# A new timetable for GpSimd's gathers in a recommender kernel with self-attention (one Trainium2 core)

## What is computed

```python
embed_x = emb_table[X + offsets[None, :]]          # 2048 x 39 x 64, the gather
att = embed_x
for i in range(3):
    q, k, v = att @ WQ[i], att @ WK[i], att @ WV[i]    # two heads of 32
    attn = softmax(einsum('bihd,bjhd->bhij', q, k))
    att = relu(einsum('bhij,bjhd->bihd', attn, v) + att @ WR[i])
att_output = relu(att.reshape(2048, 2496) @ Wlin)
h = relu(embed_x.reshape(2048, 2496) @ W1 + b1)
h = relu(h @ W2 + b2)
y = sigmoid(att_output + relu(h @ W3 + b3))
```

## Time and profile before

| | |
|---|---|
| three runs | 2014.25, 2020.08, 2020.95 us (median 2020.08, mean 2018.4) |
| the profiled execution | 2015.38 us |
| its span, first to last instruction | 2013.2 us |
| TensorE, VectorE, ScalarE, GpSimd busy | 95%, 84%, 68%, 45% of the span |
| mean granted clock of TensorE | 0.992 of full |

### The profile page before, as it was taken

The page is one execution under the profiler, slowest core; times in us unless marked ns, Lnnn a source line. Parts: engine busy times, 40 slices in busy tenths (PEclk is TensorE's granted clock), DMA queues, the critical chain, the costliest instruction groups (busy, mean ns, idle before and its releaser), DMA issues.

```text
span 2013.2 us, 105402 instructions
## 1 busy us (share of the span) xinstructions
PE 1903.5 (95%) x44960; PEld 1688.1 (84%) x44960; DVE 1691.6 (84%) x3771; ACT 1370.4 (68%) x3993; POOL 900.1 (45%) x949
## 2 busy tenths in 40 slices
PE   1598999999999999999999999999999999999998
PEld 0487888888888888888888888888888888888887
DVE  4476989888898888889888898988889888888987
ACT  2365767777777677777767677677767777777675
POOL 7553354544545454454544445454454545444000
PEclk9899999999999999999999999999999999999998
DMA  4111111111111111111111111111111111111000
GB/s 137 43 28 25 32 27 32 29 30 32 29 33 29 31 30 30 31 28 33 28 31 30 30 34 28 32 30 30 31 30 33 28 32 28 31 31 25 21 19 17
DMA packets 67862, 64.73 MB, mean 32 GB/s; under 512 B 24056, under 2 KB 54792, under 8 KB 67400
## 3 DMA queue, kind: packets, MB, share of 16 engines
q1 hardware_dynamic: 47432, 37.52, 6.4%
q0 software_dynamic: 19968, 20.49, 5.3%
HBM read 27.24 MB, written 0.01 MB: 14 GB/s over the span
## 4 chain that ended last, share of the span: by engine, by line
PE 87%; DVE 5%; issue 3%; POOL 2%; ACT 2%; another core or an unknown queue 1%; DMA 0%; ACTq 0%
PE SV L478 20%; PE Ob L495 14%; PE X L464 13%; PE X L457 8%; PE X L459 5%; PE X L458 5%; PE Mb L432 3%; PE Mb L433 3%; PE Mb L434 3%; PE Ob L457 3%; PE Ob L459 3%; PE Ob L458 3%; POOL emb L355 2%; PE Ob L423 2%; PE Mb L450 1%
## 5 line engine op out<-in xcount | busy, mean ns | idle before, releaser
L355 POOL DMA_INDIRECT emb<-L_rec_emb_table,idx_t x624 | 653.0, 1046 | 727.3 <-PE Ob L495 531.6
L742 DVE TENSOR_REDUCE den<-sd 103x16 f32<-103x624 f32 x384 | 308.2, 803 | 212.5 <-ACT sd L615 188.9
L478 PE MATMUL SV<-yv,xs 64*39 64x142 f32 x12288 | 454.5, 286 | 12.0 <-ACT v_sb L618 10.0
L478 PEld LDWEIGHTS SV<-yv,xs 64*39 64x39 f32 x12288 | 344.9, 113 | 52.4 <-issue 15.7
L722 DVE TENSOR_REDUCE mx<-SV 103x8 f32<-103x312 f32 x768 | 333.1, 475 | 33.0 <-PE SV L478 17.2
L495 PEld LDWEIGHTS Ob<-pt,v_sb 39*32 39x32 f32 x12288 | 271.7, 106 | 96.1 <-issue 95.8
L599 ACT ACTIVATE xs<-Ob 128x312 f32<-128x312 f32 x256 | 110.4, 431 | 346.4 <-PE Ob L495 345.3
L464 PE MATMUL X<-ident,pn 103*103 103x103 f32 x3072 | 342.7, 254 | 0.0
L332 POOL COPY xs<-embT 64x256 f32<-64x256 f32 x300 | 239.9, 800 | 211.8 <-ACT embT L559 77.6
L727 DVE TENSOR_TENSOR sd<-SV,mx 103x312 f32<-103x312 f32 x768 | 331.5, 474 | 0.1
L495 PE MATMUL Ob<-pt,v_sb 39*32 39x39 f32 x12288 | 324.9, 198 | 6.2 <-issue 5.9
(11 more groups left out here) (81 smaller groups left out, 2757.7 us busy)
## 6 DMA issues: line engine op xcount, KB each, us to landing
v_x<-v_sb SPq DMA_DIRECT2D x768, 39.0 KB
emb<-L_rec_emb_table,idx_t POOLq DMA_INDIRECT x624
xs<-L_rec_W SPq DMA_DIRECT2D x19, 256.0 KB
w<-L_rec_W SPq DMA_DIRECT2D x1, 512.0 KB
idx_in<-r_X SPq DMA_DIRECT2D x1, 312.0 KB, 4.0
b_b<-L_rec_b SPq DMA_DIRECT2D x1, 256.0 KB
b_b<-L_rec_b SPq DMA_DIRECT2D x1, 128.0 KB
w_b<-L_rec_W SPq DMA_DIRECT2D x1, 128.0 KB
```

Source lines behind the costliest of these rows:

```text
L355: nc.gpsimd.indirect_dma_start(out=emb[:, n % ER, f % 2 * D:(f % 2 + 1) * D], out_offset=None, in_=table, in_offset=bass.IndirectOffsetOnA ...
L478: last = nc.tensor.matmul(SV[64 * b:64 * b + F, at:at + YR], x_pair(u, e, p), yv[64 * e:64 * e + D, l, p, :], start=True, stop=True, skip_ ...
L742: nc.vector.tensor_reduce(den[:], pe_sb[:], AX.X, ALU.add).then_inc(den_ready, 1)
```

## The change

The two tables of fields are changed, tile 0 gets a table of its own for the copies, and in steps 0 to 2 of tile 0 POOL waits for the scores of the step before (`sv_ps`) before it gathers:

```diff
-    FIELDS_AT = [2, 2, 2, 2, 2, 2, 2, 2, 1, 2, 0, 2, 0, 2, 2, 0, 2, 2, 2, 0, 2, 2, 2, 2]
-    FIRST_FIELDS_AT = [10] + 9 * [2] + [1, 2, 1, 2, 2, 1, 2]
+    FIELDS_AT = [2, 2, 2, 2, 3, 2, 2, 2, 0, 2, 0, 2, 0, 2, 2, 0, 2, 2, 2, 0, 2, 2, 2, 2]
+    FIRST_FIELDS_AT = 3 * [4] + 5 * [3] + [0, 2, 0, 2, 2, 0, 2, 2, 2]
     SHUFFLE_AT = {8: 0, 10: 1, 12: 2, 15: 3, 19: 4}
+    FIRST_SHUFFLE_AT = {8: 0, 10: 1, 13: 2, 19: 3, 21: 4}
...
             for s in range(TOTAL):
                 t, ts = tile_step(s)
+                if s <= PV_AT:
+                    at_least(pool, sv_ps, 2 * s)
                 at_least(pool, o_ps, s - PV_AT)
                 for f in fields_at(s)[1]:
                     gather(fields_at(s)[0], f)
-                shuffles = ts in SHUFFLE_AT and t + 1 < TILES
-                if shuffles:
+                shuffle_at = SHUFFLE_AT if t else FIRST_SHUFFLE_AT
+                if ts in shuffle_at and t + 1 < TILES:
                     for back in range(min(4, s + 1)):
                         for f in fields_at(s - back)[1]:
                             landed(pool, fields_at(s - back)[0], f)
-                    shuffle_for(t + 1, SHUFFLE_AT[ts])
+                    shuffle_for(t + 1, shuffle_at[ts])
```

## The result

The changed kernel takes 1991.97 us (median of four runs, 1987.01 to 1997.73), the kernel before beside it 2018.65: a ratio of 0.987 (95% interval 0.9852 to 0.9889), 27 us. The forecast was 1988.0 with a range of 1975 to 2005, faster by over 0.3%. That is right. The profiled execution took 1989.57 us, 25.8 less than that of before, where the sum had said 30.4. The last experiments set a limit to what it is right about: on another chip, the third of those used here, the same change is worth 0.2%.

A forecast was written before the change was run, and what follows sets the result against it. TensorE was taken to bound the kernel (busy 95%, 87% of the chain), stalled by gather issues. Terms -14.7 + 8.4 - 8.0 - 0.7 + 1.0 - 18.1 + 1.75 = -30.4 us gave 1985.0, predicted median 1988 us, range 1975 to 2005.

The forecast's parts named there:

- Step 9, tiles 1 to 14: Without step 8's gather, copies end earlier and step 9's gathers end ahead of TensorE's burst: -14.7 us.
- Third gather in step 4: Step 8's gather, moved to step 4, ends at phase 3.30 inside the burst: 0.60 each, +8.4 us over 14 tiles.
- Tile 0, steps 0 and 1: Four gathers a step, waiting for the previous step's scores, replace fourteen issued back to back: -8.0 us.
- Tile 0, steps 9 to 23: Copies placed after their last chunk, so gathers no longer go out in bunches: -18.1 us, step 21 priced separately.
- Step 21: Tile 0's one step keeping gathers and copies together: ScalarE's cast for tile 1 comes late, +1.75 us.
- Tile 0, steps 2 to 7: Step 2: -0.7 us; third gathers in steps 3 to 7 end ahead of the burst, costing only +1.0, in step 3.
- The signs: Expected trace marks, including step 4 at about 5.4 us and PE's unnamed wait on L495 from 23.3 to about 10.
- the first: Rival: the burst's gaps are not the gathers' doing, so time stays at 2018 to 2020 us; 5%.
- A third gather costs 1.26 everywhere: Rival: step 9's stall price in all 19 steps with a third gather, sum -15.9, 2002.5 us; 10%.
- The slower case: Third gathers in step 4 and tile 0's steps 3 to 7 cost 2.4 us or more each, over 0.3% slower; 3%.
- while GpSimd issues a gather, TensorE's densest stream of small instructions does not get on: Claimed mechanism at burst L495 (64 tiny matmuls): loss grows with the issue's reach, 0.48 to 1.26 us a step.
- the rule that spoke against the change: Only VectorE and GpSimd share a port pair, so TensorE and ScalarE never wait there; sum would be about nothing.

The follow-up runs named there:

- the change's steady part alone: Kernel before with only the new FIELDS_AT table for tiles 1 to 15, tile 0 as before: 2009.97 us, ratio 0.9956.
- the kernel with the new tile 0 alone: Changed kernel with the old FIELDS_AT, keeping tile 0's tables and the sv_ps waits: 2001.39 us, ratio 0.9908.

## Why the prediction was right, and where not

- **Step 9, tiles 1 to 14**: -14.7 forecast, -15.6 measured. The early copies and the second gather ahead of the burst are as described; the change's steady part alone shows it.
- **Third gather in step 4**: +8.4 forecast, +10.7 measured, 0.76 each for 0.60. That it costs was right, the straight line between two rows too low: they were taken from second gathers, and a third costs more at the same phase. That the cost goes by how far the issue reaches into the burst was wrong, as the third gather in step 3 shows.
- **Step 10**, for which nothing was counted, fell by 3.0 us (from 71.6). 1.4 of them are a lower clock in one tile: in tile 7 the kernel before ran this step at a granted clock of 0.74 and took 6.44 us. In most others it is about 0.15 shorter, as steps behind a stalled one are longer elsewhere too (step 4 above, behind step 3's third gather); why is not shown. With 3.0 us more in small differences, tiles 1 to 14 come to -10.9, where -6.3 was forecast.
- **Tile 0, steps 0 and 1**: 10.49 us forecast, 10.73 measured.
- **Tile 0, steps 9 to 23**: 75.1 us forecast (91.46-18.1+1.75), 76.1 measured. Step 21 is the late one, 6.73 us, and the clock is 1.00 in the whole stretch, where it was 0.94.
- **Tile 0, steps 2 to 7**: here the working failed. "Where the pair takes 0.94 each, the third runs from phase 1.91 to 2.85, ahead of the burst at 2.98: nothing" gave +1.0 for steps 3 to 7; steps 3 to 8 rose by 4.9 us, from 29.3 to 34.2. The third gathers make 3.3 of it, 0.5 to 0.7 in each of their five steps and 0.2 in step 8 behind them: so it is in the kernel with the new tile 0 alone, whose clock is 1.00 there (32.54). The other 1.7 are this execution's: step 3 ran at a granted clock of 0.74 and took 6.43 us with TensorE busy throughout, and step 4 took 6.18, where the kernel with tile 0 alone has 5.51 and 5.48. The four gathers of step 2 were priced at nothing beside a gain of 0.7; the step rose by 1.1, to 7.44. The variant with the third gather in step 3 shows the same without tile 0: ending before the burst does not make a third gather free.
- **The sum**: span -25.6 us = 3.5 before the first mark, -17.0 in tile 0, -10.9 in tiles 1 to 14, -1.2 behind. The 3.5 are chance: three kernels with the same instructions there reach the first mark at 68.14, 70.47 and 74.11 us. That the total came within 5 us is partly luck: tile 0 gave 7.0 us less than the terms for it, and tiles 1 to 14 gave 4.6 more, most of it from steps that no term stood for.
- **The signs**: PE's unnamed wait was to fall to about 10 us and fell to 14.2; step 4 takes 5.6 and not 5.4. The late cast behind step 21 is there, 1.8 us for 1.75.

Of the rivals, the first falls on the first chip (the loss moved with the gathers, three times). "A third gather costs 1.26 everywhere" falls by its size (0.58 and 0.76, with the step behind it 0.76 and 0.85), but is right that the stretch ahead of the burst is not free. The slower case, from 2.4 us for each third gather on, is further off still. What I read as a property of the machine, "while GpSimd issues a gather, TensorE's densest stream of small instructions does not get on", is one of a chip: the same instructions at the same phases leave the burst whole on the third. It is too narrow even on the first, where a stop can begin after the issue has ended, VectorE waits with TensorE, and in tile 0 ScalarE does (last section). On the third chip the rule that spoke against the change, from the Trainium skill, "SBUF — State Buffer", section "SBUF: two separate sides", agrees with the rows, and its sum of "about nothing" is about what the change is worth there (0.2%). On the first chip that sum fails; whether the rule does is not shown, as no trace places the stall at the ports of the SBUF.

What stays open: what in the first chip couples a gather to TensorE and its signals. It is hardly the way that one program was loaded, since all six traces counted with it have late rises of `sv_ps`, each of another kernel, and none of the eight others has; but the kernels ran on one chip at a time, so another condition of that time is not excluded. What the number of bytes does is open too: the kernel with a quarter of them ran only where there is no stall. So is why a third gather costs at phase 2.86 and a second at 2.72 does not.

## What to carry to other kernels

Cut the profile at a mark in each step and compare the same step's sum over all tiles: a loss of one microsecond in one step of 24 is plain there, and invisible in an engine's share. Keep a queue that waits for its own transfers away from work that must start early, but price a moved instruction by rows with the same number of neighbours, not only the same phase. And profile the kernel before on a second chip before a stall without a releaser is called a rule: here 27 us of gain on one chip are 3 on another.

## What the hardware showed that was not expected

- The same program differs by 56 us between chips (2019.25 and 1963.21). The granted clock differs by too little for it: its mean is 0.992 on the first and 0.997 on the third. The two profiled executions of the kernel before differ by 50.8: 26.5 us lie in tile 0 (145.5 and 119.0) and 24.9 in tiles 1 to 14 (1670.9 and 1646.0), with 0.7 the other way outside them. Of the 24.9 step 9 makes 11.0 and step 10 6.7. Tile 8's steps 0 to 8 differ by 0.4 in 44.
- GpSimd itself is not slower on the first chip: an issue takes 0.94 us, 0.30 from one to the next, and 1.4 to 1.6 in certain places of a step, on both; the mean over all 624 is 1046 ns on both.
- In step 1 of tile 0 on the first chip ScalarE waited 9.23 us while the gathers went out, but not for a product that was late in TensorE's rows: the last of step 1's products ended at 72.08, and ScalarE's two copies of them start at 77.91 and 80.69. TensorE then stood 9.24 us for the scores, which need the copies. On the third chip, with the gathers going out just as densely, the products of the two copies end at 69.77 and 70.20 and the copies start at 69.86 and 70.23. TensorE on the first chip:

```profile
71.78 0.30 PE L459 MATMUL X<-x_hi,w_hi 128*128 128x312 f32 x1
...
82.13 2.13 PE L478 MATMUL SV<-yv,xs 64*39 64x142 f32 x32 [9.24 <-ACT v_sb L618]
```
